# Attention without a maximum: the inverses of the softmax sums handled one group or one load later

## The reference

```
Q = (x @ W_k.T), split in 16 heads
scores = -(|q_s|^2 - 2 q_s.q_t + |q_t|^2) / sqrt(8)
attn = softmax(scores); context = attn @ Q
out = (context @ merged) / sqrt(8) @ W_o.T
```

## Time and profile before

| | us |
|---|---|
| three timed executions | 1774.29, 1771.08, 1762.38 (median 1771.08) |
| profiled execution, its own time | 1770.14 |
| its span | 1768.3 |
| TensorE busy | 1577.2 (89%) |
| ScalarE busy | 1281.8 (72%) |
| VectorE busy | 1199.9 (68%) |
| GpSimd busy | 546.5 (31%) |
| mean granted TensorE clock | 0.938 |

### The profile page before, as it was taken

How to read it: one execution, slowest core, us unless ns; L and a number is a source line. 1 busy time by engine, 2 the same in 40 slices (tenths; PEclk the granted TensorE clock), 3 DMA queues, 4 the chain that set the end, 5 groups by cost and what they waited for, 6 DMA issues and landing times. The chain is left out here.

```text
span 1768.3 us, 38427 instructions
## 1 busy us (share of the span) xinstructions
PE 1577.2 (89%) x14142; PEld 741.9 (42%) x14142; DVE 1199.9 (68%) x2379; ACT 1281.8 (72%) x2177; POOL 546.5 (31%) x940
## 2 busy tenths in 40 slices
PE   7889996874999999989798999878877999999998
PEld 4667575652233333237433333244441333333256
DVE  4777777798999999958500000036669999999843
ACT  4654653796588888876698998747764888888863
POOL 3422422642223333325300000023332233333462
PEclk9998988886899999999999999989985999999999
DMA  4000000035434333410233222211234233333211
GB/s 128 1 1 1 1 1 1 1 116 168 120 102 109 105 105 108 109 31 26 60 99 86 88 84 87 65 28 50 82 97 114 74 92 91 86 89 90 65 34 41
DMA packets 140414, 125.45 MB, mean 71 GB/s; under 512 B 38410, under 2 KB 118340, under 8 KB 140228
## 3 DMA queue, kind: packets, MB, share of 16 engines
q1 hardware_dynamic: 130980, 121.90, 23.9%
q0 software_dynamic: 8192, 0.77, 0.9%
q10 hardware_dynamic: 1056, 0.33, 0.1%
HBM read 77.19 MB, written 44.96 MB: 69 GB/s over the span
## 5 line engine op out<-in xcount | busy, mean ns | idle before, releaser
L1665 ACT ACTIVATE m_probs<-m_psum 128x512 f32<-128x512 f32 (+1 forms) x768 | 513.5, 760 | 93.1 <-PE m_psum L1601 92.5
L1665 ACT ACTIVATE e_probs<-e_psum 128x512 f32<-128x512 f32 x512 | 277.3, 597 | 63.7 <-PE e_psum L1601 61.9
L1709 DVE TENSOR_REDUCE a_minus_max<-e_psum 128x1 f32<-128x512 f32 x512 | 315.8, 682 | 9.6 <-PE e_psum L1610 4.0
L1709 DVE TENSOR_REDUCE a_minus_max<-m_psum 128x1 f32<-128x512 f32 x512 | 316.4, 681 | 8.1 <-PE m_psum L1610 1.3
L1601 PE MATMUL m_psum<-m_q_stack,m_k_stack 114*32 114x512 bf16 (+1 forms) x4096 | 298.8, 388 | 7.7 <-DMA m_k_stack<-n_parts 4.3
L1621 PE MATMUL m_psum<-m_probs,m_v_ones 128*32 128x512 f32 x2048 | 274.8, 609 | 21.0 <-DVE m_pair L1655 19.0
L1601 PEld LDWEIGHTS m_psum<-m_q_stack,m_k_stack 114*32 114x32 bf16 (+1 forms) x4096 | 108.3, 97 | 228.7 <-issue 115.7
L1601 PE MATMUL e_psum<-e_q_stack,e_k_stack 126*32 126x512 bf16 x2048 | 158.2, 385 | 2.2 <-ACT e_probs L1665 2.2
L1621 PE MATMUL e_psum<-e_probs,e_v_ones 128*32 128x512 f32 x1024 | 132.7, 593 | 1.9 <-POOL e_v_ones L1555 1.0
L1610 PE MATMUL m_psum<-m_k_stack,m_q_stack 48*128 48x512 bf16 x512 | 112.7, 399 | 17.2 <-DVE a_minus_max L1709 16.9
L1610 PE MATMUL e_psum<-e_k_stack,e_q_stack 60*128 60x512 bf16 x512 | 113.4, 401 | 11.4 <-DVE a_minus_max L1709 11.1
(11 more groups left out here) (403 smaller groups left out, 2686.0 us busy)
## 6 DMA issues: line engine op xcount, KB each, us to landing
polar_q<-m_late SPq DMA_DIRECT2D x24, 256.0 KB, 3.0
polar_k<-m_late SPq DMA_DIRECT2D x24, 256.0 KB, 3.3
m_q_stack<-polar_q SPq DMA_DIRECT2D x64, 96.0 KB, 2.3
m_k_stack<-polar_k SPq DMA_DIRECT2D x64, 96.0 KB, 2.4
ctx<-a_context_pairs SPq DMA_DIRECT2D x48, 128.0 KB
a_context_pairs<-slot_w SPq DMA_DIRECT2D x24, 256.0 KB, 2.4
m_q_stack<-dist_parts SPq DMA_DIRECT2D x192, 32.0 KB
m_k_stack<-dist_parts SPq DMA_DIRECT2D x192, 32.0 KB
```

The lines of the kernel that those rows point to most:

```text
L1665: act.activation(self.buf.probs[(NT * m + c) % self.buf.PROBS][:, self.WIDE * part:self.WIDE * (part + 1), :], self.ps_s[i % self.PAIRS], ...
L1709: dve.tensor_reduce(self.minus_max[n % 2][:, k:k + 1], ps[:, :], AX.X, ALU.max, negate=True).then_inc(self.bank_free, 1)
```

## The change

`invert` moves from VectorE's step 4b + 4 to step 4b + 5. On SyncE `keep` moves from `contexts_soon(4b + 4)` to `contexts_soon(4b + 5)`, and `spread_out` to `contexts_soon(4b + 6)`, where it stands ahead of that step's send. GpSimd's `scale_context(b)` moves from step 4b + 7 to step 4b + 8, and the one for b = 6 follows the loop.

```diff
     def contexts_soon(self, sp, s):
 
+        if s >= 5 and s % 4 == 1:
+            self.context.keep(sp, s // 4 - 1, s // 4 - 1)
+        if s >= 6 and s % 4 == 2:
+            self.context.spread_out(sp, s // 4 - 1, s // 4 - 1)
         if s >= 2 and s % 2 == 0:
             self.send(sp, s // 2 - 1)
             self.fetch(sp, s // 2 - 1)
-        if s >= 4 and s % 4 == 0:
-            self.context.keep(sp, s // 4 - 1, s // 4 - 1)
-            self.context.spread_out(sp, s // 4 - 1, s // 4 - 1)
...
-        if not self.with_max and s >= 7 and s % 4 == 3:
-            self.scale_context(pool, s // 4 - 1)
+        if not self.with_max and s >= 8 and s % 4 == 0:
+            self.scale_context(pool, s // 4 - 2)
...
-        if not self.with_max and c == 0 and s >= 4 and s % 4 == 0:
+        if not self.with_max and c == 0 and s >= 5 and s % 4 == 1:
             self.invert(dve, s // 4 - 1)
...
                 for s in range(N):
                     second.gpsimd(pool, s)
+                second.scale_context(pool, NB - 2)
```

## The result

| | median us | lowest to highest | ratio to before, 95% interval |
|---|---|---|---|
| before, 4 runs | 1769.7 | 1762.4 to 1774.3 | |
| changed kernel, 4 runs | 1750.8 | 1749.3 to 1751.7 | 0.9896 [0.9861, 0.9931] |
| changed kernel, timed again later beside before (1769.5) | 1745.9 | 1743.0 to 1746.8 | 0.9859 [0.9836, 0.9881] |

The changed kernel is 1.0 to 1.4% faster.

What follows compares the result with a forecast made beforehand. SyncE's queue was taken to bound the second attention (a5), 32.6 us a cycle against 29.3. From 1770.1, 23.8 us gone (16.9 TensorE's waits, 6.9 slower clock) gives 1746.3; with 1 us for a slow send, 1747 us, range 1739 to 1758.

Steps and rivals of the forecast that it cites:

- The bound: Second attention (a5) turns at SyncE's pace: 32.6 us from reciprocal to reciprocal, 32.9 on average, against 29.3 wanted.
- Part 1: VectorE in a5: the reciprocal one group later leaves the instruction order the same; worth nothing.
- Part 2: SyncE's queue in a5: keep and spread each one load later; both waits go, 5.0 us in four groups.
- The cycle: SyncE's turn for four groups: loads 19.1, sends and fetches 4.35 and 3.43, keep and spread 1.0; sum 27.9 us.
- the loads: SyncE's loads in a5: four take 19.1 us; with the waits gone they come earlier and stay ahead of TensorE.
- the bound of 5.6: SyncE's send directly behind the spread: upper bound 5.6 us, where 3.25 was taken.
- The start: First cycles of a5: the first reciprocal's 2.2 us stall stays; the second reciprocal, at 957.6, fits by 1.1 us.
- Part 3: GpSimd in a5: multiplication behind one more copy of values; cost 0, or 7.7 us in all if cover were gone.
- SyncE will wait for scores: SyncE's queue in later cycles of a5: once caught up, it waits for scores instead, harmlessly.
- The sum: a5: 21.7 and 2.1 us gone, together 23.8; 1 us left for one slow send at the second reciprocal.
- It arrives whole: End of a5: all engines meet there, so the stage's 23.8 us gain reaches the total time whole.
- The half case: Rival, 20%: SyncE's cycle stays above 29.3, at 31.0 us; total about 1759, in a milder case 1751.

Runs made afterwards that it cites:

- parts 1 and 3 alone: Changed kernel with SyncE's order put back, so only VectorE's reciprocal and GpSimd's multiplication stand later; 1768.5 us, ratio 0.9994 to before.
- only reciprocal behind the copy: Kernel before with only VectorE's reciprocal moved behind the next pair's copy (step 4b+6); SyncE and GpSimd as before; 1759.9 us, ratio 0.9950.

## Why the prediction was right, by its own steps

**The bound.** Right: removing SyncE's waits alone gives the whole gain, moving the spread alone gives about 3 us, VectorE's and GpSimd's parts alone none that can be measured.

**Part 1, the reciprocal one group later is worth nothing.** Right, its order on VectorE is unchanged, and the kernel with parts 1 and 3 alone is at 0.9994.

**Part 2, SyncE.** Both waits went, 26.3 to 3.7 us and 7.3 to 1.0. The cycle was mis-sized: 27.9 forecast, (1104.55 - 932.85) / 6 = 28.6 measured. The term that was too small is the loads, 2 x 9.56 = 19.1: the four loads of a cycle took 19.2 to 20.4 us, 19.7 on average. The trace of before had it already: the pair of loads taken was the shortest of twelve between 932 and 1121 us, which average 9.8 and reach 10.5. The send behind the spread was right, 3.28 to 3.40 us in five of six and 3.85 once, near the row taken (3.25), under the bound of 5.6. The Trainium skill ("DMA: Bandwidth & Descriptors", queues, rings and completion order) says that a semaphore increment lands only after every earlier write of the same DMA engine; the estimate by it was 3.6. The traces agree with the rule: in the first cycles the fetch went out 0.2 to 0.4 us behind GpSimd's start on the spread's data (971.97 behind 971.75), and with the spread behind the send it took 2.03 in the first cycle. They don't prove it, since sends with no spread ahead of them took up to 4.4 us too (1039.51 to 1043.91 before the change). This is the row of the kernel before, GpSimd's start at 1132.47, that the prediction compares with the send:

```profile
1132.47 1.27 POOL L1405 TENSOR_TENSOR ctx<-ctx,m_scale 128x512 f32<-128x512 f32 x1 [8.67 <-DMA m_scale<-a_context_inverses]
```

**The start.** The first stall was forecast at 2.2 and measured 2.2. The second reciprocal was to fit by 1.1 us: the copy came 962.59 - 961.55 = 1.04 behind its start; less the 0.47 that the reciprocal needs, the room was 0.6 (1.0 in the second trace, 958.11 - 956.65 = 1.46). The kernel with keep and spread behind one load, whose second reciprocal came late, shows what a miss costs: a stage 4.4 us longer.

**Part 3 and the loads.** Right, no wait of TensorE for either. "SyncE will wait for scores" was wrong for the changed kernel: at 28.6 it gains only 0.7 us a cycle on TensorE, too little to catch up within seven. It changes nothing in the time.

**The sum.** 23.8 us forecast, 24.5 in a5's trace: 16.8 of TensorE's waits (19.0 less 2.2; 16.9 forecast) and 7.7 of slower clock (6.9 forecast). The 1 us kept for a slow send wasn't needed. 1747 forecast; 1750.8 and 1745.9 measured. "It arrives whole" was not quite so, with 2 us more in the last group. The two timings of the changed kernel lie 4.9 us apart, of which their traces show 4.4 ahead of a5 (first copy at 901.77 and 897.38), so how near 1747 came to either is in part luck; the sum is judged by the 24.5 us of a5. The half case did not come: no average stayed over 29.3. Single cycles did go over, 29.5 (1047.29 to 1076.80) in the first trace and 30.6 (984.67 to 1015.22) in the second; the lead won before paid for them.

## What to carry to other kernels

Add up a DMA-issuing queue like an engine: issues, and every wait between them, per turn of the loop, against the turn's own pace; here 32.9 against 29.3 us although nothing on the queue shows as busy. If the queue is the bound, take out the wait that is a round trip (fetch, compute, write back) by putting independent issues between its two ends. Moving only the consumer out of the way turns the stall into another one as soon as buffered work is used up: 10 us gained instead of 24.

## What the hardware showed that was not expected

How long TensorE stood did not settle alone what clock it had afterwards. In the ten traces it kept its full clock behind every stall for a pair's copy of up to 2.2 us (the interval to the next copy is 14.60 us), and lost some of it behind all but two of those from 2.46 us up. Two stalls of one trace, keep and spread behind one load, show it: behind the one of 2.56 us the interval was 14.60 us, behind that of 2.46 us it was 16.18, with the mean granted clock at 0.89. The other exception is one of 2.54 us with the spread behind the send. (Columns as in the result: the third from the right is the granted clock.)

```profile
931.57:946.17 14.60, 13.83 (x184) 5.17 (x188) 0.62 (x2) 12.29 (x14) 1.51 (x2) 1.00 0.32 94
963.33:979.51 16.18, 15.41 (x184) 6.09 (x188) 0.62 (x2) 12.40 (x14) 1.57 (x2) 0.89 0.34 102
```

A stall for a load of 1.65 us (only reciprocal behind the copy, at 1001.65 us) was followed by a granted clock of 0.73 over 6.4 us. So a short stall can cost more than its own length: of the 24.5 us gained, 7.7 are such slower stretches and not waits.
